# Routed sweep of an expert layer: the down weights are split inside the expert's own piece, between its up blocks

## Chip, cores and metric

One core of one Trainium2 chip. The metric is the device time of one execution of the whole kernel in microseconds; the times shown are the median of several executions, and the profile is of one execution more.

## What is computed

The reference normalises `x` (8 x 1024 tokens of 512 channels), runs a gated linear recurrence over it, and multiplies it by the SiLU of a mixture of 32 experts. What matters here is the routed part of that mixture:

```python
topk_ids = jnp.argmax(logits, axis=-1)             # one expert for each token
order = jnp.argsort(topk_ids)
sorted_x = (x * sigmoid(topk_val))[order]
g = ragged_dot(sorted_x, routed_gate_w, tokens_per_expert)   # 512 -> 1024
u = ragged_dot(sorted_x, routed_up_w, tokens_per_expert)     # 512 -> 1024
d = ragged_dot(silu(g) * u, routed_down_w, tokens_per_expert)  # 1024 -> 512
```

All values are float32. The kernel gets its precision by writing every operand as a rounded part `hi` plus a remainder `lo` and summing three products: hi x hi, hi x lo and lo x hi.

## The kernel before

The kernel has three sweeps, one after the other: the shared part of the mixture, the recurrence, and `routed_sweep`, which the change touches. The routed sweep fills the last third of the time, from about 2615 us of the profiled execution.

**Pieces.** The routed sweep walks over pieces. A piece is up to 384 tokens of one expert, as 8, 10 or 12 units of 32 tokens, so its matmuls have 256, 320 or 384 columns. An expert with more than 384 tokens has `full` whole pieces ahead of its last one; `full` is read from a table while the kernel runs, as are the number `p` of the first piece and the size `n` of the last. The last piece of an expert goes through `piece(p + full, e, n, split)`.

**What TensorE (PE) does in a piece.** There are eight blocks `b` of 128 hidden channels each. For each block it forms the gate product into `tG` (lines 87 to 89, 12 matmuls) and then the up product into `tU` (12 matmuls); each of the two has two banks, used in turn. Before the gate product of block b it waits for `sg_done`, that is for the SiLU of block b-2 on ScalarE (L1413), and before the up product for `h_done`, the product of block b-2 on VectorE (L1494). After block 6 it transposes the first 128 tokens of the piece that follows (`turn_x(p + 1, 0)`, L1558, into the one buffer `tX`). Then comes the down product (L1601), with two halves of the hidden channels: `down(0, 0)`, `turn_x(p + 1, 1)`, `down(0, 1)`, for a piece of more than 256 tokens `down(0, 2)`, then `turn_x(p + 1, 2)` or, where the next piece has only two groups of tokens, a bare wait in its place, and `down(1, g)` for all groups. Each `turn_x` waits until VectorE has emptied `tX` of the group before (`xlo`).

**What ScalarE (ACT) and VectorE (DVE) do in a piece.** For each block ACT computes `silu(b)` (L1413), DVE the product `h_mul(b)` (L1494), ACT the rounded copy `h_hi(b)` (L1422), DVE the remainder `h_lo(b)` (L1498). Both engines work strictly in the order in which the code lists the instructions. In block 7 the first transposed group is split too: ACT `x_hi` (L1401), DVE `x_lo` (L1469).

**The weights.** An expert's weights are six parts q of 1 MB each: q = 0 to 3 hold the gate and up columns of two blocks each, q = 4 (`D0`) and q = 5 (`D1`) the two halves of the down weights. A part is loaded by SyncE's queue (L1260, two transfers of 512 KB) into `raw[q % 3]`; ACT rounds it into `whi[q]` (`split_hi`, L1284), DVE takes the remainder into `wlo[q]` (`split_lo`, L1288). SyncE loads the parts in the order 0 to 5 and waits before each until the part three places earlier has been split, since that frees the raw buffer. `whi` and `wlo` have one buffer for each part.

**Where the splits stand.** Ahead of the sweep all six parts of expert 0 are split. In a piece of expert e (its last one) the parts of expert e+1 are split: q = 0 after block 2, q = 1 after block 4, on ACT q = 2 in block 6 and q = 3 after block 7, on DVE both after block 7; then `D0` after the x splits, and `D1` at the very end, after the output work of the piece (`gated`, L1452 on ACT; `total` and `result`, L1508, L1512 and L1515 on DVE). The next piece begins on ACT and DVE with register work: three table values (`order`, L1205) are read.

**The output** of a piece: DVE adds the shared part to `psY`, ACT takes the SiLU, DVE multiplies and adds, and GpSimd scatters the rows.

Of the kernel before, what the change touches and what calls it, by code (L numbers as in the profile page):

```python
# [1119 lines left out]
def routed_sweep(nc, z, x, rgw, ruw, rdw, xs_dram, ss_dram, tok_dram, orders, listed, ident, out):  # L1120
# [5 lines left out]
    KD, NI, D, E, T, NU = z.KD, z.NI, z.D, z.E, z.T, z.NU  # L1126
    GROUPS = PIECE // P
# [13 lines left out]
    with ExitStack() as ctx:  # L1141
# [84 lines left out]
            with eng.Else():  # L1226
                by_size(eng, n, body, sizes[:half])

        def experts(eng, piece):


            def expert(e, split):
                p = order(eng, FIRST_PIECE, e, 0, E + MOST)
                full = order(eng, FULL, e, 0, MOST)
                n = order(eng, LAST, e, LEAST, MOST_UNITS)
                with eng.If(full > 0):
                    with eng.Fori(0, MOST) as i:
                        with eng.If(full > i):
                            piece(p + i, e, MOST_UNITS, False)
                piece(p + full, e, n, split)  # L1240

            with eng.Fori(0, E - 1) as e:
                expert(e, True)
            expert(E - 1, False)

        def part(q, e):

# [34 lines left out]
        def split_hi(act, q, e):  # L1282
            act.wait_ge(raw_loaded[q], (e + 1) * 32)
            act.activation(whi[q][:], raw[q % RING][:], ACT.Copy).then_inc(whi_done[q], 1)  # L1284

        def split_lo(dve, q, e):
            dve.wait_ge(whi_done[q], e + 1)
            dve.tensor_tensor(wlo[q][:], raw[q % RING][:], whi[q][:], ALU.subtract).then_inc(wlo_done[q], 1)  # L1288
# [106 lines left out]
        @block.scalar  # L1395
        def _(act):
            act.sem_inc(sg_done, 2)

            def x_hi(p, g):
                act.wait_ge(turned_x, p * GROUPS + g + 1)  # L1400
                act.activation(xT[:, 0, :, turned(g)], psX[:], ACT.Copy).then_inc(xhi, 1)  # L1401

            split_hi(act, 0, 0)
            for g in range(GROUPS):
                x_hi(0, g)
            for q in range(1, PARTS):
                split_hi(act, q, 0)

            def piece(p, e, n, split):
                def silu(b):  # L1410
                    act.wait_ge(g_mm, p * NI + b + 1)
                    act.wait_ge(h_done, p * NI + b + 1)
                    act.activation(sg[b % 2][:], psG[b % 2][:, 0:PIECE], ACT.Silu).then_inc(sg_done, 1)  # L1413

                def h_hi(b):
                    act.wait_ge(h_done, p * NI + b + 3)
                    if b < KH:
                        act.wait_ge(d0_mm, p * 2 + 2)
                    else:
                        for g in range(GROUPS):  # L1420
                            act.wait_ge(y_mm[g], p + 1)
                    act.activation(hT[:, 0, b], h[b % 2][:], ACT.Copy).then_inc(hhi, 1)  # L1422

                def hi(q):
                    if split:
                        if q < D0:
                            act.wait_ge(u_mm, p * NI + 2 * q + 2)
                        elif q == D0:
                            act.wait_ge(d0_mm, p * 2 + 4)
                        else:  # L1430
                            for g in range(GROUPS):
                                act.wait_ge(y_mm[g], p + 2)
                        split_hi(act, q, e + 1)

                for b in range(NI):
                    silu(b)
                    if b == NI - 2:
                        hi(2)
                    if b == NI - 1:
                        act.wait_ge(u_mm, p * NI + NI)  # L1440
                        x_hi(p + 1, 0)
                    h_hi(b)
                    if b == 2 or b == 4:
                        hi(b // 2 - 1)
                hi(NQ - 1)
                for g in range(1, GROUPS):
                    x_hi(p + 1, g)
                hi(D0)

                def gated(g):  # L1450
                    act.wait_ge(z_done[g], p + 2)
                    act.activation(yo[g][:], yo[g][:], ACT.Silu).then_inc(zs_done[g], 1)  # L1452

                gated(0)
                gated(1)
                third(act, n, lambda: gated(2), lambda: act.sem_inc(zs_done[2], 1))
                hi(D1)

            experts(act, piece)

        @block.vector
        def _(dve):
            dve.sem_inc(h_done, 2)
            for g in range(GROUPS):
                dve.sem_inc(z_done[g], 1)

            def x_lo(p, g):
                dve.wait_ge(xhi, p * GROUPS + g + 1)
                dve.tensor_tensor(xT[:, 1, :, turned(g)], psX[:], xT[:, 0, :, turned(g)], ALU.subtract).then_inc(xlo, 1)  # L1469

            by_step = [t[:, 0:NU].rearrange("p (s n) -> p n s", n=STEP) for t in (scatter_at, gather_at)]
            numbers = psY[0][:, 0:NU].rearrange("p (n s) -> p n s", n=STEP)
            for bank in psG + psU:
                dve.memset(bank[:], 0.0).then_inc(cleared, 1)
            dve.wait_ge(returned, 16 * STEP)
            dve.tensor_copy(back, back_i).then_inc(back_done, 1)
            dve.wait_ge(turned_table, 1)
            dve.tensor_copy(by_step[0], numbers).then_inc(table, 1)
            dve.tensor_scalar(clipped, psY[0][:, 0:NU], float(T - 1), None, ALU.min).then_inc(table, 1)
            dve.memset(gather_at[:, NU:NU + 16], 0)  # L1480
            dve.memset(scatter_at[:, NU:NU + 16], T).then_inc(table, 1)
            dve.wait_ge(table, 3)
            dve.tensor_copy(by_step[1], clipped.rearrange("p (n s) -> p n s", n=STEP)).then_inc(table, 1)
            split_lo(dve, 0, 0)
            for g in range(GROUPS):
                x_lo(0, g)
            for q in range(1, PARTS):
                split_lo(dve, q, 0)

            def piece(p, e, n, split):  # L1490
                def h_mul(b):
                    dve.wait_ge(sg_done, p * NI + b + 3)
                    dve.wait_ge(u_mm, p * NI + b + 1)
                    dve.tensor_tensor(h[b % 2][:], sg[b % 2][:], psU[b % 2][:, 0:PIECE], ALU.mult).then_inc(h_done, 1)  # L1494

                def h_lo(b):
                    dve.wait_ge(hhi, p * NI + b + 1)
                    dve.tensor_tensor(hT[:, 1, b], h[b % 2][:], hT[:, 0, b], ALU.subtract).then_inc(hlo, 1)  # L1498

                def lo(q):  # L1500
                    if split:
                        split_lo(dve, q, e + 1)

                def total(g):
                    dve.wait_ge(y_mm[g], p + 2)
                    dve.wait_ge(ss_loaded[g], (p + 1) * 16)
                    dve.wait_ge(yo_free, p + 1)
                    dve.tensor_tensor(yo[g][:], psY[g][:], ss[g][:, 0:D], ALU.add).then_inc(z_done[g], 1)  # L1508

                def result(g):  # L1510
                    dve.wait_ge(zs_done[g], p + 1)
                    dve.tensor_tensor(yo[g][:], yo[g][:], ss[g][:, D:2 * D], ALU.mult).then_inc(zm_done[g], 1)  # L1512
                    dve.wait_ge(zm_done[g], p + 1)
                    dve.wait_ge(xr_loaded[g], (p + 1) * 16)
                    dve.tensor_tensor(yo[g][:], yo[g][:], xr[g][:], ALU.add).then_inc(yo_done[g], 1)  # L1515

                for b in range(NI):
                    h_mul(b)
                    if b == NI - 1:
                        x_lo(p + 1, 0)  # L1520
                    h_lo(b)
                    if b == 2 or b == 4:
                        lo(b // 2 - 1)
                lo(2)
                x_lo(p + 1, 1)
                lo(NQ - 1)
                x_lo(p + 1, 2)
                lo(D0)

                def absent():  # L1530
                    dve.sem_inc(z_done[2], 1)
                    dve.sem_inc(zm_done[2], 1)
                    dve.sem_inc(yo_done[2], 1)

                def last():
                    total(2)
                    result(2)

                total(0)
                total(1)  # L1540
                result(0)
                result(1)
                third(dve, n, last, absent)
                lo(D1)

            experts(dve, piece)

        @block.tensor
        def _(pe):
# [127 lines left out]
```

## Time and profile before

| | |
|---|---|
| median of 3 executions | 4001.32 us (3999.62 to 4002.64) |
| the profiled execution, own time | 3997.86 us |
| its span, first to last instruction | 3996.2 us |
| PE busy | 3867.3 us, 97% |
| DVE busy | 2083.3 us, 52% |
| ACT busy | 2018.7 us, 51% |
| mean granted TensorE clock | 0.988 |

The span leaves out what lies before the first and after the last instruction, 1.7 us here. Busy time of PE is the union of its matmuls, whose ends are modelled. A row of the timeline gives start, duration, engine, line, operation, the tile written and the tiles read, and in square brackets how long the engine had been idle before it and what ended that.

### The profile page before, as it was taken

The page shows a single profiled execution, that of the slowest core. Times are in us where ns is not written, and L with a number is a line of the kernel's source. Part 1 is how long each engine was busy: PE and PEld are TensorE (multiplying, and loading weights), DVE is VectorE, ACT ScalarE, POOL GpSimd, SP SyncE. Part 2 cuts the span into 40 slices and gives each one's busy share as a digit, 9 for nine tenths or more (in the row PEclk, how much of TensorE's full clock was granted, in tenths as well). Part 3 has the DMA queues.
Part 4 walks back from the last instruction along what each step waited for, and adds up shares of the span by engine and source line. Part 5 has one row for each costly group of instructions (what it writes and reads, how often), then busy time and mean ns, then how long its engine had stood idle before and what let it go on. Part 6 is the DMA issues. An engine that isn't in the chain of part 4 may idle for free. (4 is left out here: it accounts for less than half of the span.)

```text
span 3996.2 us, 57408 instructions
## 1 busy us (share of the span) xinstructions
PE 3867.3 (97%) x19586; PEld 3290.6 (82%) x19587; DVE 2083.3 (52%) x3048; ACT 2018.7 (51%) x2696; POOL 790.7 (20%) x840
## 2 busy tenths in 40 slices
PE   7999999999989999999999999959999999999998
PEld 5888888888867788888888888858999999998997
DVE  5232322323246655555555555556667767677674
ACT  3222222222227666676666666645455556555553
POOL 2011010111103200000000000024333434343433
PEclk9999999999989999999999999979999999999999
DMA  4212121121122000000010000066676767777673
GB/s 157 76 74 84 59 88 63 79 79 73 64 62 66 32 32 32 31 31 31 32 63 31 31 31 31 10 211 223 215 246 229 262 219 257 239 263 250 219 264 125
DMA packets 271955, 466.38 MB, mean 117 GB/s; under 512 B 23306, under 2 KB 171403, under 8 KB 268052
## 3 DMA queue, kind: packets, MB, share of 16 engines
q1 hardware_dynamic: 234276, 346.48, 25.3%
q0 software_dynamic: 37616, 119.08, 8.6%
q8 instruction: 37, 0.61, 0.1%
q14 instruction: 26, 0.21, 0.0%
HBM read 364.73 MB, written 102.99 MB: 117 GB/s over the span
## 5 line engine op out<-in xcount | busy, mean ns | idle before, releaser
L87 PE MATMUL gate<-xT,w_hi 128*128 128x512 f32 x1536 | 600.6, 391 | 1.9 <-DVE b2all L990 1.9
L88 PE MATMUL gate<-xT,w_hi 128*128 128x512 f32 x1536 | 600.5, 391 | 0.0
L89 PE MATMUL gate<-xT,w_lo 128*128 128x512 f32 x1536 | 598.9, 390 | 0.0
L1288 DVE TENSOR_TENSOR wlo<-raw,whi 128x2048 fp32r<-128x2048 f32 x192 | 439.6, 2289 | 127.8 <-ACT whi L1284 127.7
L529 DVE TENSOR_TENSOR h_act<-h_act,psU 128x512 f32<-128x512 f32 x128 | 88.0, 687 | 683.9 <-PE psU L89 683.8
L1601 PE MATMUL tY<-whi,thT 128*128 128x512 f32 x1264 | 410.7, 395 | 2.6 <-issue 2.4
L1284 ACT ACTIVATE whi<-raw 128x2048 fp32r<-128x2048 f32 x192 | 365.4, 1903 | 46.0 <-DMA raw<-in_L_ffn_routed_up_w 26.1
L87 PEld LDWEIGHTS gate<-xT,w_hi 128*128 128x128 f32 x1536 | 288.7, 188 | 67.1 <-DVE b2all L990 3.5
L89 PEld LDWEIGHTS gate<-xT,w_lo 128*128 128x128 f32 x1536 | 288.9, 188 | 62.1
L88 PEld LDWEIGHTS gate<-xT,w_hi 128*128 128x128 f32 x1536 | 288.7, 188 | 60.5
L87 PE MATMUL tG<-txT,whi 128*128 128x256 f32 (+2 forms) x1024 | 309.2, 302 | 25.6 <-ACT tsg L1413 12.8
L1034 DVE SCALAR_TENSOR_TENSOR log_f<-gate,b1s,log_f 128x512 f32<-128x512 f32 x128 | 96.1, 751 | 407.3 <-ACT log_f L931 407.3
L87 PE MATMUL tU<-txT,whi 128*128 128x256 f32 (+2 forms) x1024 | 305.7, 299 | 2.5 <-DVE th L1494 2.5
L89 PE MATMUL tG<-txT,wlo 128*128 128x256 f32 (+2 forms) x1024 | 304.9, 298 | 0.0
L88 PE MATMUL tG<-txT,whi 128*128 128x256 f32 (+2 forms) x1024 | 304.8, 298 | 0.0
L88 PE MATMUL tU<-txT,whi 128*128 128x256 f32 (+2 forms) x1024 | 304.7, 298 | 0.0
L89 PE MATMUL tU<-txT,wlo 128*128 128x256 f32 (+2 forms) x1024 | 304.6, 298 | 0.0
L1422 ACT ACTIVATE thT<-th 128x384 fp32r<-128x384 f32 x256 | 134.0, 523 | 302.8 <-DVE th L1494 302.8
L884 POOL COPY state<-hs 128x1 f32<-128x1 f32 x128 | 23.7, 185 | 1320.8 <-DVE hs L965 1320.8
L1601 PEld LDWEIGHTS tY<-whi,thT 128*128 128x128 f32 x1264 | 237.4, 188 | 54.3 <-issue 6.5
L431 ACT ACTIVATE h_act<-psG 128x512 f32<-128x512 f32 x128 | 76.5, 598 | 347.2 <-PE psG L89 345.4
L1601 PE MATMUL tY<-wlo,thT 128*128 128x512 f32 x632 | 246.4, 390 | 0.0
(210 smaller groups left out, 8913.4 us busy)
## 6 DMA issues: line engine op xcount, KB each, us to landing
raw<-in_L_ffn_routed_gate_w SPq DMA_DIRECT2D x128, 512.0 KB, 3.7
raw<-in_L_ffn_routed_up_w SPq DMA_DIRECT2D x128, 512.0 KB, 4.7
raw<-in_L_ffn_routed_down_w SPq DMA_DIRECT2D x128, 512.0 KB, 4.7
xT_dram<-xT SPq DMA_DIRECT2D x16, 2048.0 KB, 6.3
xT<-xT_dram SPq DMA_DIRECT2D x14, 2048.0 KB, 8.1
x_in<-in_L_attn_x SPq DMA_DIRECT2D x16, 1024.0 KB, 5.4
xs_dram<-x_in SPq DMA_DIRECT2D x16, 1024.0 KB
ss_dram<-y_sb SPq DMA_DIRECT2D x64, 256.0 KB, 2.1
```

Source lines behind the costliest of these rows:

```text
L87: pe.matmul(out, w[0], x[0], start=start, stop=False)
L88: pe.matmul(out, w[0], x[1], start=False, stop=False)
L89: return pe.matmul(out, w[1], x[0], start=False, stop=stop)
L431: act.activation(h[:, b % 2], psG[b % 2][:], ACT.Silu).then_inc(sg_done, 1)
L529: dve.tensor_tensor(h[:, b % 2], h[:, b % 2], psU[b % 2][:], ALU.mult).then_inc(h_done, 1)
L884: pool.tensor_copy(state[:, kb:kb + 1], hs[:, CHUNK - 1:CHUNK]).then_inc(state_done, 1)
L1034: dve.scalar_tensor_tensor(lf[:], bank(n, 0)[:], bias(GF, kb), lf[:], ALU.add, ALU.min)\
L1284: act.activation(whi[q][:], raw[q % RING][:], ACT.Copy).then_inc(whi_done[q], 1)
L1288: dve.tensor_tensor(wlo[q][:], raw[q % RING][:], whi[q][:], ALU.subtract).then_inc(wlo_done[q], 1)
L1422: act.activation(hT[:, 0, b], h[b % 2][:], ACT.Copy).then_inc(hhi, 1)
L1601: mm = pe.matmul(psY[g][:], hT[:, a, b, g * P:(g + 1) * P], w[q][:, kb, :], start=b == 0 and a == 0 and w is whi, stop=b == NI - 1 and a == 1)
```

## The change

On ACT and DVE the splits of the down parts D0 and D1 leave the end of the piece of the expert ahead. They are done in the expert's own first piece, D0 after block 0 and D1 after block 2 (`own_half`, under a branch on `full < 1`; where the expert has full pieces, they are done in front of these instead). The gate and up parts of the next expert move too: q = 0 from after block 2 to after block 3, q = 1 from after block 4 to after block 5, q = 2 on ACT from block 6 to after block 7; and the x splits of groups 1 and 2 stand now between q = 2 and q = 3 (ACT) or around q = 2 (DVE). Ahead of the sweep only q = 0 to 3 of expert 0 are split. The code of TensorE, SyncE and GpSimd is unchanged.

```diff
-        def experts(eng, piece):
+        def experts(eng, piece, own):
...
                 with eng.If(full > 0):
+                    for q in (D0, D1):
+                        own(p, e, q)
                     with eng.Fori(0, MOST) as i:
                         with eng.If(full > i):
-                            piece(p + i, e, MOST_UNITS, False)
-                piece(p + full, e, n, split)
+                            piece(p + i, e, MOST_UNITS, False, None)
+                piece(p + full, e, n, split, full)
...
+        def own_half(eng, own, p, e, q, full):
+            if full is not None:
+                with eng.If(full < 1):
+                    own(p, e, q)
...
@@ scalar
-            for q in range(1, PARTS):
+            for q in range(1, NQ):
                 split_hi(act, q, 0)
+            def own(p, e, q):
+                if q == D0:
+                    act.wait_ge(d0_mm, p * 2 + 2)
+                else:
+                    for g in range(GROUPS):
+                        act.wait_ge(y_mm[g], p + 1)
+                split_hi(act, q, e)
...
                 def hi(q):
                     if split:
-                        if q < D0:
-                            act.wait_ge(u_mm, p * NI + 2 * q + 2)
-                        elif q == D0:
-                            act.wait_ge(d0_mm, p * 2 + 4)
-                        else:
-                            for g in range(GROUPS):
-                                act.wait_ge(y_mm[g], p + 2)
+                        act.wait_ge(u_mm, p * NI + 2 * q + 2)
                         split_hi(act, q, e + 1)
                 for b in range(NI):
                     silu(b)
-                    if b == NI - 2:
-                        hi(2)
                     if b == NI - 1:
                         act.wait_ge(u_mm, p * NI + NI)
                         x_hi(p + 1, 0)
                     h_hi(b)
-                    if b == 2 or b == 4:
+                    if b == 0 or b == 2:
+                        own_half(act, own, p, e, D0 + b // 2, full)
+                    if b == 3 or b == 5:
                         hi(b // 2 - 1)
+                hi(2)
+                x_hi(p + 1, 1)
                 hi(NQ - 1)
-                for g in range(1, GROUPS):
-                    x_hi(p + 1, g)
-                hi(D0)
+                x_hi(p + 1, 2)
...
                 third(act, n, lambda: gated(2), lambda: act.sem_inc(zs_done[2], 1))
-                hi(D1)
@@ vector
-            for q in range(1, PARTS):
+            for q in range(1, NQ):
                 split_lo(dve, q, 0)
+            def own(p, e, q):
+                split_lo(dve, q, e)
...
                     h_lo(b)
-                    if b == 2 or b == 4:
+                    if b == 0 or b == 2:
+                        own_half(dve, own, p, e, D0 + b // 2, full)
+                    if b == 3 or b == 5:
                         lo(b // 2 - 1)
+                x_lo(p + 1, 1)
                 lo(2)
-                x_lo(p + 1, 1)
+                x_lo(p + 1, 2)
                 lo(NQ - 1)
-                x_lo(p + 1, 2)
-                lo(D0)
...
                 third(dve, n, last, absent)
-                lo(D1)
```

## Rows read from the trace of the kernel before

**Rows 1.** The page: span, and each engine's busy time, share, instructions.

```profile
span 3996.2 us, 57408 instructions
...
PE 3867.3 (97%) x19586; PEld 3290.6 (82%) x19587; DVE 2083.3 (52%) x3048; ACT 2018.7 (51%) x2696; POOL 790.7 (20%) x840
```

**Rows 2.** PE's waits from 2500 us on: total us, times, longest us.

```profile
PE tG L87 <- ACT tsg L1413: 12.8, 8, 7.5
...
PE tX L1558 <- DVE txT L1469: 8.7, 18, 1.5
...
PE tU L87 <- DVE th L1494: 2.5, 9, 0.3
```

**Rows 3.** Groups of PE by shape, from 2620 us on: first gate matmuls.

```profile
L87 PE MATMUL tG<-txT,whi 128*128 128x256 f32 x544 | 157.9, 290 | 22.1 <-ACT tsg L1413 12.8 <-issue 9.3
...
L87 PE MATMUL tG<-txT,whi 128*128 128x320 f32 x416 | 129.7, 312 | 3.5 <-issue 3.5
```

**Rows 4.** ACT's timeline in a piece of 256 columns, from its blocks.

```profile
3130.23 0.53 ACT L1422 ACTIVATE thT<-th 128x384 fp32r<-128x384 f32 x1 [1.55 <-DVE th L1494]
...
3133.47 0.52 ACT L1422 ACTIVATE thT<-th 128x384 fp32r<-128x384 f32 x1 [0.71 <-DVE th L1494]
3133.90 1.90 ACT L1284 ACTIVATE whi<-raw 128x2048 fp32r<-128x2048 f32 x1
3135.70 0.47 ACT L1413 ACTIVATE tsg<-tG 128x384 f32<-128x384 f32 x1
3138.62 0.52 ACT L1422 ACTIVATE thT<-th 128x384 fp32r<-128x384 f32 x1 [2.45 <-DVE th L1494]
...
3148.14 0.51 ACT L1422 ACTIVATE thT<-th 128x384 fp32r<-128x384 f32 x1
```

**Rows 5.** DVE's timeline, the same piece: its start, the first split.

```profile
3125.91 0.69 DVE L1515 TENSOR_TENSOR yo<-yo,xr 128x512 f32<-128x512 f32 x1
3126.51 2.29 DVE L1288 TENSOR_TENSOR wlo<-raw,whi 128x2048 fp32r<-128x2048 f32 x1
3129.56 0.55 DVE L1494 TENSOR_TENSOR th<-tsg,tU 128x384 f32<-128x384 f32 x1 [0.76 <-PE tU L89]
...
3135.82 2.29 DVE L1288 TENSOR_TENSOR wlo<-raw,whi 128x2048 fp32r<-128x2048 f32 x1 [1.25 <-ACT whi L1284]
```

**Rows 6.** PE's timeline: blocks 0 and 1 of that piece, its second transpose.

```profile
3123.05 0.28 PE L87 MATMUL tG<-txT,whi 128*128 128x256 f32 x1
...
3125.93 0.28 PE L87 MATMUL tG<-txT,whi 128*128 128x256 f32 x1
...
3150.36 0.66 PE L1558 MATMUL tX<-ident,xg 128*128 128x128 f32 x4 [0.36 <-DVE txT L1469]
```

**Rows 7.** PE's and ACT's timelines, the piece of 320 columns at 3205 us.

```profile
3205.57 0.30 PE L87 MATMUL tG<-txT,whi 128*128 128x320 f32 x1
...
3236.92 0.60 PE L1558 MATMUL tX<-ident,xg 128*128 128x128 f32 x4
...
3213.17 0.52 ACT L1422 ACTIVATE thT<-th 128x384 fp32r<-128x384 f32 x1 [0.97 <-DVE th L1494]
```

**Rows 8.** Timelines at the first piece: PE, then DVE.

```profile
2682.35 0.60 PE L1558 MATMUL tX<-ident,xg 128*128 128x128 f32 x4
...
2648.46 2.29 DVE L1288 TENSOR_TENSOR wlo<-raw,whi 128x2048 fp32r<-128x2048 f32 x1 [0.57 <-ACT whi L1284]
...
2656.49 2.29 DVE L1288 TENSOR_TENSOR wlo<-raw,whi 128x2048 fp32r<-128x2048 f32 x1 [2.62 <-ACT whi L1284]
2659.87 0.56 DVE L1494 TENSOR_TENSOR th<-tsg,tU 128x384 f32<-128x384 f32 x1 [1.08 <-ACT tsg L1413]
```

**Rows 9.** A stretch: us, busy time of each engine, PE clock, DMA share, GB/s.

```profile
2660.00:2670.00 10.00, 10.00 (x66) 10.00 (x66) 5.40 (x8) 4.51 (x7) 3.69 (x4) 0.74 0.95 345
```

**Rows 10.** ACT's table loads at L1413: duration min/median/max, first and last start.

```profile
L1413 ACT ACT_TABLE_LOAD  x31: 1283/1283/1283, 2657.3 to 3901.5; - x31
```

**Rows 11.** SyncE's queue, its waits from 2500 us on.

```profile
SPq L1260 <- DVE wlo L1288: 1076.5, 188, 12.9
```

More of the change, by code:

```diff
@@ L1405, in _, with piece @@
                 x_hi(0, g)
-            for q in range(1, PARTS):
+            for q in range(1, NQ):
                 split_hi(act, q, 0)
-            def piece(p, e, n, split):
+            def own(p, e, q):
[5 more added lines that the diff above has]
+                split_hi(act, q, e)
+            def piece(p, e, n, split, full):
                 def silu(b):
@@ L1456, in piece @@
                 third(act, n, lambda: gated(2), lambda: act.sem_inc(zs_done[2], 1))
-                hi(D1)
-            experts(act, piece)
+            experts(act, piece, own)
         @block.vector
@@ L1486, in _, with piece @@
                 x_lo(0, g)
-            for q in range(1, PARTS):
+            for q in range(1, NQ):
                 split_lo(dve, q, 0)
-            def piece(p, e, n, split):
+            def own(p, e, q):
+                split_lo(dve, q, e)
+            def piece(p, e, n, split, full):
                 def h_mul(b):
@@ L1543, in piece @@
                 third(dve, n, last, absent)
-                lo(D1)
-            experts(dve, piece)
+            experts(dve, piece, own)
         @block.tensor
```

## The prediction

> **What bounds the kernel now.** I read the page first: PE is busy for 97% of the span, ACT and DVE for about half of it [rows 1]. The kernel is bound by matmuls, and a change to ACT's and DVE's order can do two things only: take away waits of PE, or make new ones. So the next view is the list of what PE waits for from the last part of the recurrence on [rows 2]. The three waits that the change can reach are those for the SiLU (12.8 us, of which 7.5 are one wait in the first piece), for the emptied `tX` (8.7 us) and for `h_mul` (2.5 us): 24 us in all, and that is the ceiling of any gain, save for a clock effect below. Then I look at how large the pieces are. A piece has 8 x 4 = 32 gate matmuls of line 87, so the groups by shape give 544/32 = 17 pieces of 256 columns and 416/32 = 13 of 320 [rows 3]; with 32 experts and no expert in two pieces, the other 2 have 384. So `full` is 0 for all experts, and each piece will split its own down parts in its blocks 0 and 2. Last comes the timeline of one 256-column piece, where the answer lies [rows 4 to 6]. All times in it are counted from its first gate matmul at 3123.05.
>
> **The change, part by part.** The number of splits stays: 192 on each engine, none longer or shorter. The output work, the matmuls and the bytes loaded are the same. What changes is how many splits stand between the blocks.
>
> *A block with a split behind it.* ACT and DVE form one chain there: `h_hi(2)` starts at 3133.47, ACT's split at 3133.90 (1.90 us), DVE's at 3135.82 (2.29 us), only then can DVE do `h_mul(3)`, and `h_hi(3)` starts at 3138.62. From `h_hi` to `h_hi` that is 5.15 us [rows 4, 5]. Without a split it is 1.62: `h_hi(0)` at 3130.23, `h_hi(2)` at 3133.47, 3.24 for two [rows 4]. PE needs 2.88 us for a block of 256 columns (3123.05 to 3125.93 [rows 6]) and may be two blocks ahead of the chain, no more, since `tG` and `tU` have two banks.
>
> *Before*, the chain has two splits up to block 6. `h_hi(0)` starts at 7.18, `h_hi(6)` at 25.09 [rows 4], and `turn_x(p+1, 1)`, which needs the `x_lo` of block 7, at 27.31 after a wait of 0.36 [rows 6], 2.22 behind `h_hi(6)`. So in these pieces chain and PE are nearly level already.
>
> *After*, there are four: behind blocks 0 (D0), 2 (D1), 3 and 5. The chain is then 4 x 5.15 + 2 x 1.62 = 23.84 from `h_hi(0)` to `h_hi(6)`, and 26.06 with the 2.22 to `turn_x`. With `h_hi(0)` at 7.18 as before, `turn_x` starts at 33.24 and not at 27.31. That is 5.93 us late, and what PE does behind it (the rest of the down product) is its own work and comes later by as much. I count the piece by this one point because the waits inside it are all included: walking PE along the chain I get waits of about 1.2 us at the gate product of block 3 (it needs `silu(1)`, which stands behind the D0 split: 7.18 + 0.43 + 1.80 + 0.47 = 9.9, against 8.7), 1.0 at the up product of block 3 (`h_mul(1)` ends at 12.3), 0.9 at the up product of block 5, 1.3 and 1.0 at the two of block 6, and 1.4 at `turn_x`: 6.8, less the 0.65 or so of before, is the same again within 0.3. Of 17 such pieces 16 pay this (the first is worked out below): 16 x 5.93 = 94.9 us.
>
> *Pieces of 320 columns.* `turn_x` starts at 3236.92 - 3205.57 = 31.35, with no wait, and `h_hi(0)` at 7.60 [rows 7]. After: 7.60 + 26.06 = 33.66, 2.31 late. Where the piece ahead has only two groups of tokens, `h_hi(0)` can start as early as 7.18, which makes it 1.89. I take 2.1. The last piece splits only D0 and D1 and keeps its slack, so 12 pieces pay: 25.2 us. A piece of 384 columns needs about 384/320 of the block time, some 5.6 us more up to `turn_x`, and its chain is no longer: nothing.
>
> *The first piece.* Before, `silu(0)` and `h_mul(0)` stand behind the splits of D0 and D1: `h_mul(0)` starts at 2659.87, 3.38 after the last split's start at 2656.49. After, the last split ahead is that of q = 3, at 2648.46, so `h_mul(0)` can start at 2651.84, `h_hi(0)` at 2652.42, and with the chain of four splits `turn_x` at 2678.48. Before it started at 2682.35 [rows 8]. The 7.5 us wait goes, the splits between the blocks take half of it back: -3.9 us.
>
> *The start of the other pieces.* One split (D1) no longer stands between the output work and `silu(0)`, and D0 is gone from the down phase. I count this at nothing, since another thing covers it: the read of three table values, which goes on while that split runs. The split starts at 3126.51, 0.60 after the last output instruction's start, and `h_mul(0)` only at 3129.56, 0.76 after DVE is free again [rows 5]. Without the split these reads begin at most 0.6 sooner: bound -0.6 x 28 = -17 us. Against it stands the new branch, twice a piece on each engine, whose cost no row shows by itself. On DVE it lies in the 1.9 us in which DVE waits for `whi`; on ACT beside the 0.43 us of `h_hi`. From below it costs nothing; from above I set for both branches of a piece together the 0.76 that DVE loses at a piece's start, where it reads three table values and takes several branches [rows 5]: 28 x 0.76 = +21 us. Nearest is the place itself, under the 0.43 and the 1.9 us of cover, so I take zero for both.
>
> *Loads.* SyncE's code is the same, its waits move with the splits. They come late now by the dozen (1076.5 us in 188 waits [rows 11]), so the queue is idle for most of a piece. The shortest path after the change is q = 3: its raw buffer comes free in block 3 and it is needed after block 7, over 15 us for 1 MB; D1's comes free in the down phase and is needed after block 2. Nothing.
>
> **Sum.** 94.9 + 25.2 - 3.9 = 116.2 us. The profiled execution took 3997.9 us (span 3996.2), so 4114 for one like it; the median of the runs shown is 3.5 us longer: 4117 us.
>
> **A rule on the clock.** After the one wait of 7.5 us the granted clock was 0.74 in the stretch that followed [rows 9], a mixture of the two levels, 1.2 and 2.4 GHz; the other seven waits for the SiLU are (12.8 - 7.5) / 7 = 0.8 us each [rows 2], and the mean over the whole execution is 0.988, so they cannot each have cost such a stretch. The new waits are at most 1.4 us long but come six to a piece. The Trainium skill, "TensorE: Matmul & The Clock Gate", section "A second HAM failure mode: psum-queue depth-cycling", says that an engine that idles shortly and often between groups of matmuls can swing between both levels. No stretch here shows that; if it held, it is the second rival below.
>
> **The rivals.**
> - *The lead of PE swallows the splits* (faster). Place: between `h_hi(0)` and `turn_x` of each piece. It decides if the two more splits cost that chain nothing: 27.31 - 7.18 = 20.13 us are there, and 17.91 + 2.22 = 20.13 are used, with a wait of 0.36 already. Then PE would lose its waits for SiLU, `tX` and `h_mul`, up to 24 us less the first wait's share, and about 2.5 us more for the slow clock behind the first wait: 3981 at best. Against it: 5.15 between `h_hi` and `h_hi` with a split is the sum of its parts, 0.43 + 1.92 + 2.2 + 0.6, and it is made of instructions that wait for each other. 0.05.
> - *The clock swings* in the 256-column pieces: 0.74 over 10 us is 2.6 us lost; 16 x 2.6 = 42 on top: 4159. 0.04.
> - *Half is hidden*: were the 320-column pieces to pay nothing, and the 256-column ones half, because the chain catches up in blocks 6 and 7 more than it does in [rows 4], the sum is 47 - 4 = 43: 4045. For it speaks only that the chain was never seen with more than two splits; against it the same as above. 0.06.
> - *Nothing measurable*, the loss of the pieces being as small as the gain of the first: 4001. 0.02.
> - *A table load at each branch.* ACT loads its table once a piece (31 times 1283 ns [rows 10]). If the new branches made it load again before `silu(1)` and `silu(3)`, that SiLU would end 3.6 us after the split's start, and DVE is free of its own split only after 4.1: mostly hidden, within the range.
>
> **How the numbers follow.** The forecast has 0.83. Its own bounds are the -17 and +21 of the start and the branches, and 2.1 for 320 columns between 1.9 and 2.3 (12 x 0.2 = 2.4 either way): 4117 - 19 = 4098 to 4117 + 23 = 4140. Of the other cases those below lie far off; to leave out no more than 2 in 10 I go a little beyond these bounds, from 4085 to 4143. Faster and slower mean by more than 0.2% (8 us), about what a measurement of this kernel can tell from no change: faster 0.05, within 0.02, slower 0.93.
>
> **What would show it.** In the changed kernel's profile a 256-column piece should last 5.9 us longer than before, with `h_hi(0)` to `h_hi(1)` at 5.15, and `turn_x` at 33 behind the piece's first matmul; a 320-column piece some 2 us longer, a 384-column piece as long as before. PE's wait for `h_mul` should grow from 2.5 us to some 55, that for the SiLU to some 45, that for `tX` to some 30. The wait of 7.5 in the first piece should be gone. I am wrong if a piece starts much sooner than now (then the register work was no cover), if ACT and DVE step faster than 5.15 with a split, or if a wait for `whi` or for a raw buffer turns up.

## The result and the profile after

The changed kernel takes 4104.72 us (4102.65 to 4105.91, 4 runs) where the kernel before takes 4000.47 (3998.09 to 4002.64) in runs beside it. The ratio is 1.0263, with a 95% interval of 1.025 to 1.0276: 104 us slower. The forecast was 4117, 12 us too high. The profiled execution took 4105.19 us.

The page of the changed kernel:

```profile
span 4103.5 us, 57600 instructions
...
PE 3893.3 (95%) x19584; PEld 3294.7 (80%) x19587; DVE 2082.9 (51%) x3048; ACT 2013.3 (49%) x2696; POOL 800.9 (20%) x840
```

Beside [rows 1] the span is 107.3 us longer, and the counts and busy times of DVE and ACT are as they were, within 6 us. So none of their work became longer. PE waits more. Its waits from 2500 us on, in total, with their number and the longest:

```profile
PE tU L87 <- DVE th L1508: 41.1, 62, 0.7
PE tG L87 <- ACT tsg L1431: 37.9, 52, 1.1
PE tX L1572 <- DVE txT L1480: 29.6, 29, 1.5
```

These three were 2.5, 12.8 and 8.7 us [rows 2]; 24.0 have become 108.6, which is 85 of the 107 us. The other part stands in PE's busy time, 26 us longer with the same matmuls: busy time is counted to the modelled ends, and a wait begins there only. Where the waits come from is seen in one piece, the same one as in [rows 4 to 6]; its first gate product is now at 3149.36. ACT's timeline, `h_hi` (L1440) and the table load ahead of the first SiLU:

```profile
3153.06 1.28 ACT L1431 ACT_TABLE_LOAD   x1 [2.15 <-issue]
...
3156.54 0.53 ACT L1440 ACTIVATE thT<-th 128x384 fp32r<-128x384 f32 x1 [1.70 <-DVE th L1508]
3156.97 1.90 ACT L1294 ACTIVATE whi<-raw 128x2048 fp32r<-128x2048 f32 x1
...
3161.70 0.52 ACT L1440 ACTIVATE thT<-th 128x384 fp32r<-128x384 f32 x1 [2.45 <-DVE th L1508]
...
3163.31 0.52 ACT L1440 ACTIVATE thT<-th 128x384 fp32r<-128x384 f32 x1 [0.71 <-DVE th L1508]
...
3168.46 0.53 ACT L1440 ACTIVATE thT<-th 128x384 fp32r<-128x384 f32 x1 [2.45 <-DVE th L1508]
...
3173.76 0.52 ACT L1440 ACTIVATE thT<-th 128x384 fp32r<-128x384 f32 x1 [2.60 <-DVE th L1508]
3175.38 0.52 ACT L1440 ACTIVATE thT<-th 128x384 fp32r<-128x384 f32 x1 [0.71 <-DVE th L1508]
3180.53 0.53 ACT L1440 ACTIVATE thT<-th 128x384 fp32r<-128x384 f32 x1 [2.45 <-DVE th L1508]
```

From `h_hi(0)` to `h_hi(6)` the steps are 5.16, 1.61, 5.15, 5.30, 1.62 and 5.15: 23.99 us, where 17.91 were spent before [rows 4]. Each 5 us step has one split in it. PE's timeline of the piece:

```profile
3149.36 0.28 PE L87 MATMUL tG<-txT,whi 128*128 128x256 f32 x1
...
3161.72 0.38 PE L87 MATMUL tU<-txT,whi 128*128 128x256 f32 x1 [0.72 <-DVE th L1508]
...
3182.76 0.66 PE L1572 MATMUL tX<-ident,xg 128*128 128x128 f32 x4 [1.39 <-DVE txT L1480]
```

The up product of block 3 starts at 12.36 behind the first row, 0.02 after `h_hi(1)`: it waited for `h_mul(1)`. The second transpose starts at 33.40 where it was 27.31 [rows 6]. DVE's timeline, the start of the piece and `h_mul(4)`:

```profile
3152.21 0.69 DVE L1529 TENSOR_TENSOR yo<-yo,xr 128x512 f32<-128x512 f32 x1
3155.87 0.55 DVE L1508 TENSOR_TENSOR th<-tsg,tU 128x384 f32<-128x384 f32 x1 [2.97 <-PE tU L89]
...
3173.03 0.55 DVE L1508 TENSOR_TENSOR th<-tsg,tU 128x384 f32<-128x384 f32 x1
```

From the last output instruction to `h_mul(0)` it is 3.66 us; with the D1 split between them it was 3129.56 - 3125.91 = 3.65 [rows 5]. The split left and the time stayed: DVE is now idle for 2.97 of it. The one step that is 0.15 longer, behind block 3, is late at `h_hi(4)`: `h_mul(4)` ends at 3173.58 and `h_hi(4)` starts 0.18 behind that end.

I took the length of each piece from PE's timeline, from its first gate product to the next piece's, in both profiled executions. The differences make up the span's:

| what | pieces | us longer |
|---|---|---|
| 256 columns, behind a piece with two groups of tokens | 9 | 52.1 |
| 256 columns, behind a piece with three groups | 7 | 36.0 |
| 320 columns, without the last piece | 12 | 24.8 |
| 384 columns | 2 | 0.0 |
| the first piece | 1 | -3.1 |
| the last piece | 1 | 0.0 |
| what lies ahead of the first gate product (2643.77 to 2641.24) | | -2.5 |
| sum | | 107.3 |

The first piece, on PE's timeline of the changed kernel:

```profile
2641.24 0.57 PE L87 MATMUL tG<-txT,whi 128*128 128x256 f32 x1 [9.18 <-issue]
...
2653.49 0.39 PE L87 MATMUL tG<-txT,whi 128*128 128x256 f32 x1 [0.86 <-ACT tsg L1431]
...
2676.95 0.66 PE L1572 MATMUL tX<-ident,xg 128*128 128x128 f32 x4 [1.38 <-DVE txT L1480]
```

The wait of 7.5 us for the first SiLU has shrunk to 0.86, and `turn_x` starts at 2676.95 instead of 2682.35 [rows 8].

### The profile page after: what moved, and what is told of

It is laid out like the page before. It is cut to its first block and busy times, and to the rows that moved or that the text cites. A ratio compares the mean times of both kernels' runs of the same rounds, so it can differ in the third digit from the quotient of the medians.

```text
span 4103.5 us, 57600 instructions
## 1 busy us (share of the span) xinstructions
PE 3893.3 (95%) x19584; PEld 3294.7 (80%) x19587; DVE 2082.9 (51%) x3048; ACT 2013.3 (49%) x2696; POOL 800.9 (20%) x840
## 5 line engine op out<-in xcount | busy, mean ns | idle before, releaser
L1294 ACT ACTIVATE whi<-raw 128x2048 fp32r<-128x2048 f32 x192 | 364.7, 1900 | 25.6 <-DMA raw<-in_L_ffn_routed_up_w 25.6
L1440 ACT ACTIVATE thT<-th 128x384 fp32r<-128x384 f32 x256 | 134.3, 525 | 414.0 <-DVE th L1508 414.0
```

## The experiments

Each was timed beside the kernel before. The first four kernels were timed beside runs of it with a median of 3996.8 us, the other four beside 3996.2, so the ratios compare better than the times. Losses and gains by pieces come from the profiled executions, measured as in the table above.

### The same splits in pairs

```diff
-                    if b == 0 or b == 2:
-                        own_half(act, own, p, e, D0 + b // 2, full)
-                    if b == 3 or b == 5:
-                        hi(b // 2 - 1)
+                    if b == 2:
+                        own_half(act, own, p, e, D0, full)
+                        own_half(act, own, p, e, D1, full)
+                    if b == 5:
+                        hi(0)
+                        hi(1)
```

DVE likewise.

> The changed kernel with the same four splits between the blocks, but D0 and D1 both behind block 2 and q = 0 and 1 both behind block 5. Theory (the chain h_hi to h_hi sets the piece): with two splits in a row ACT's second runs beside DVE's first, so such a step takes 5.15 + 2.20 = 7.35 us and not 5.15 + 5.15 - 1.62 = 8.68 for the two; from h_hi(0) to h_hi(6) 2 x 7.35 + 4 x 1.62 = 21.2 instead of 23.84, and PE, two blocks ahead, loses some 2.7 us less in a 256-column piece (about 3 us over the kernel before) and all of the 2 us in a 320-column piece: 4105 - 16 x 2.7 - 12 x 1.9 = 4039. Rival (every split between the blocks costs PE the same, wherever it stands): 4105. Rival (the loss comes from D0 and D1 no longer being covered by the down phase, not from the chain between the blocks): 4105.

Measured: 4062.35 us (4056.36 to 4064.45), ratio 1.0165 (1.0148 to 1.0182). By the ratios (1.0263 to 1.0165) that is 39 us less than the changed kernel, where both rivals expected nothing and the theory 66. ACT's timeline of the same piece:

```profile
3138.47 0.52 ACT L1440 ACTIVATE thT<-th 128x384 fp32r<-128x384 f32 x1 [0.71 <-DVE th L1510]
3138.90 3.70 ACT L1294 ACTIVATE whi<-raw 128x2048 fp32r<-128x2048 f32 x2
...
3145.82 0.52 ACT L1440 ACTIVATE thT<-th 128x384 fp32r<-128x384 f32 x1 [2.85 <-DVE th L1510]
```

The step with two splits is 7.35 us, to the hundredth what was worked out, and the 320-column pieces lose only 6.2 us together. So the number of splits alone does not set the loss, and neither does the mere absence of D0 and D1 from the down phase. The rest of the missing gain is a thing that the theory left out. PE's timeline of that piece at `turn_x`:

```profile
3158.79 1.11 PE L1576 MATMUL tX<-ident,xg 128*128 128x128 f32 x4 [2.32 <-DVE txT L1482]
3159.56 0.78 PE L1619 MATMUL tY<-whi,thT 128*128 128x512 f32 x1
3160.13 0.63 PE L1619 MATMUL tY<-wlo,thT 128*128 128x512 f32 x1
```

and two stretches, of this kernel behind that wait of 2.32 us and behind the same wait in the piece at 3047.78:

```profile
3158.00:3163.00 5.00, 4.21 (x14) 3.56 (x15) 3.27 (x5) 3.95 (x4) 0.00 (x0) 0.66 1.06 369
...
3077.50:3082.50 5.00, 4.18 (x20) 3.43 (x21) 3.27 (x5) 4.81 (x5) 0.00 (x0) 1.00 0.88 310
```

In the first the granted clock is 0.66, part of it at the lower of the two levels (1.2 of 2.4 GHz), and the down product runs at 0.63 us for a matmul, not 0.39. In the second, behind a wait just as long, it stays at 1.00. The slow stretch is there in 11 of the 17 pieces of 256 columns. It costs some 1.5 us: pieces behind a three-group piece take 39.3 to 39.7 us without it and 40.8 to 40.9 with it, and those behind a two-group piece, nearly all with it, 41.0 to 41.5. By pieces, the 256-column pieces behind the first are 25.6 us shorter than in the changed kernel where 43 were expected, and eleven times 1.5, some 16 us, is nearly the whole of that miss. The 320-column pieces are 18.6 us shorter where 23 were expected; the first piece and what lies ahead of it are 4.5 shorter, which was not expected. So the profiled execution is 49 us faster than the changed kernel's. It was the fastest of four; the others took 5 to 8 us longer, and no trace shows why. ACT's waits for `raw`, in 13 places more than in the changed kernel and 8 us together, may have a part in what is left.

The 256-column pieces of the changed kernel, the first left aside, have no such stretch; their waits end at 1.39:

```profile
3182.00:3187.00 5.00, 4.24 (x23) 3.61 (x24) 3.27 (x5) 4.86 (x5) 0.00 (x0) 1.00 0.51 176
```

The changed kernel has one slow stretch, though, at the start of its third piece, of 320 columns, where PE stood still for 2.80 us, and not for ACT or DVE:

```profile
2731.33 0.41 PE L87 MATMUL tG<-txT,whi 128*128 128x320 f32 x1 [2.80 <-issue]
...
2731.00:2736.00 5.00, 4.67 (x21) 4.68 (x22) 0.87 (x2) 1.77 (x2) 2.27 (x2) 0.66 0.44 159
```

The kernel before stood still for 3.49 us in that place and kept its clock at 1.00.

### DVE's part of the own splits cut short

```diff
+            dve.wait_ge(whi_done[0], 1)
+            for q in (D0, D1):
+                dve.tensor_tensor(wlo[q][:], whi[0][:], whi[0][:], ALU.subtract)
...
             def own(p, e, q):
-                split_lo(dve, q, e)
+                dve.wait_ge(whi_done[q], e + 1)
+                dve.tensor_tensor(wlo[q][:, :, 0:64], raw[q % RING][:, :, 0:64], whi[q][:, :, 0:64],
+                                  ALU.subtract).then_inc(wlo_done[q], 1)
```

The first three lines set both remainders to zero once, ahead of the sweep. The kernel leaves out seven eighths of each.

> The changed kernel, with DVE's subtraction for D0 and D1 cut to an eighth of its columns (the rest of those remainders is left at zero; ACT's part, the loads and all waits stay). Theory: behind a D split h_mul waits for ACT's 1.80 us and the SiLU only, so that step falls from 5.15 to 0.43 + 1.80 + 0.50 + 0.60 = 3.35 us; 1.8 us less for each of two steps, 3.6 in a 256-column piece, and a 320-column piece loses nothing any more: 4105 - 16 x 3.6 - 12 x 1.9 = 4024. Rival (the branches or ACT's split alone set the loss): 4105, at most a few us less.

Measured: 4019.36 us (4019.29 to 4020.57), ratio 1.0056 (1.004 to 1.0073), 83 us below the same kernel with the whole subtraction, which at its ratio of 1.0263 is 4102 beside 3996.8. ACT's timeline around the first own split:

```profile
3127.84 0.53 ACT L1440 ACTIVATE thT<-th 128x384 fp32r<-128x384 f32 x1 [1.69 <-DVE th L1513]
...
3131.26 0.53 ACT L1440 ACTIVATE thT<-th 128x384 fp32r<-128x384 f32 x1 [0.71 <-DVE th L1513]
```

The step is 3.42 us instead of 5.16. The 256-column pieces behind the first lose 31.1 us instead of 88.1, which is 3.56 less each where 3.6 was expected, and those of 320 columns 0.8 instead of 24.8. ACT's splits, the branches and the loads are all still there, so the part of the loss that is gone with it belongs to DVE's subtraction, which stands in front of `h_mul`.

### Without the branches

```diff
-                with eng.If(full < 1):
-                    own(p, e, q)
+                own(p, e, q)
```

> The changed kernel without the branches around the own D splits (right only where no expert has more than 384 tokens, as here). Theory: the branches lie under h_hi and under DVE's wait for whi, so 4105 within 2 us. Rival (the new branches are part of the loss): up to 0.38 us for each of 56 on a piece's path, 4084.

Measured: 4098.44 us (4097.2 to 4099.94), ratio 1.0253 (1.0236 to 1.027). The time alone does not tell it from the changed kernel, since the intervals overlap. The trace does. ACT's `h_hi(0)` and `h_hi(6)` in the same piece:

```profile
3153.53 0.53 ACT L1439 ACTIVATE thT<-th 128x384 fp32r<-128x384 f32 x1 [1.70 <-DVE th L1507]
...
3177.36 0.53 ACT L1439 ACTIVATE thT<-th 128x384 fp32r<-128x384 f32 x1 [2.45 <-DVE th L1507]
```

They are 23.83 us apart, against 23.99 with the branches and 23.84 in the forecast. The 0.15 is gone from the step behind block 3: `h_hi(4)` starts here 0.04 behind the end of `h_mul(4)`, not 0.18. By pieces the span is 101.5 us longer than before and not 107.3: 2.3 us less in the 256-column pieces, 2.3 in those of 320, 1.5 in the first. So in the 28 pieces behind the first that lose time the branches cost 4.6 us, about 0.16 a piece, and not up to 0.76.

### Both gate and up splits behind the blocks

```diff
-                    if b == 3 or b == 5:
-                        hi(b // 2 - 1)
-                hi(2)
+                hi(0)
                 x_hi(p + 1, 1)
-                hi(NQ - 1)
+                hi(1)
                 x_hi(p + 1, 2)
+                hi(2)
+                hi(NQ - 1)
```

DVE's part moves in the same way.

> The changed kernel with q = 0 and 1 taken out from between the blocks and put behind block 7, so only D0 and D1 stand between the blocks, as many as in the kernel before, and q = 0 to 3 all follow the blocks. Theory with the down phase counted: DVE has four splits (8.8 us) and two x remainders between the last h_lo and the output work, total(0) comes some 3 us later than in the kernel before, h_hi(0) of the next piece with it, near 10 us behind the piece's start and not 7.2; the 320-column pieces lose too: about 4105 to 4110. Rival (only the number of splits between the blocks counts): that of the kernel before, about 4000.

Measured: 4146.02 us (4144.81 to 4148.36), ratio 1.0374 (1.0357 to 1.0392). As many splits between the blocks as in the kernel before, and the slowest kernel of all: the rival falls, and the theory was too mild by some 40 us. One thing that it left out is on ACT's timeline, at the last of the four:

```profile
3159.39 1.91 ACT L1294 ACTIVATE whi<-raw 128x2048 fp32r<-128x2048 f32 x1 [4.18 <-DMA raw<-in_L_ffn_routed_up_w]
```

Part q = 3 is loaded into the raw buffer that q = 0 leaves. With q = 0 split only behind block 7, its load starts there too, and ACT waits 4.18 us for it. `h_hi(0)` of the next piece is at 12.79, not near 10. The output work stands behind it, then the next piece's first SiLU, and PE's waits are in the place that the delay of `h_hi(0)` reaches:

```profile
PE tG L87 <- ACT tsg L1431: 102.6, 33, 5.1
...
PE tX L1572 <- DVE txT L1480: 1.5, 1, 1.5
```

The 320-column pieces lose 51 us here, double what they do in the changed kernel. The clock has a share too: the mean granted clock of this execution is 0.976, where it is 0.989 in the changed kernel. Between the first and the last piece it was at its lower level in 24 stretches of 3.4 or 6.8 us, 116 us together, each beginning within or just behind an idle time of PE of 2.6 to 5.1 us. At half the clock that is a loss of at most 58 us. How much of the 40 is the load's and how much the clock's was not separated.

### Three splits between the blocks

As before, but `q = 0` stays behind block 3, and only `q = 1` moves behind block 7:

```diff
-                    if b == 3 or b == 5:
-                        hi(b // 2 - 1)
+                    if b == 3:
+                        hi(0)
+                hi(1)
+                x_hi(p + 1, 1)
                 hi(2)
-                x_hi(p + 1, 1)
```

> The changed kernel with q = 1 taken from behind block 5 to behind block 7; three splits stay between the blocks. Theory: the chain is one split shorter (3.5 us), but DVE's output work comes later by a split, so the next piece's h_hi(0) moves from 7.2 to about 8; a 256-column piece loses some 1 us less than in the changed kernel: 4105 - 19 = 4086. The kernel with all four behind block 7 had also a wait for the load of q = 3; here its buffer comes free in block 3, so none is expected. Rival (each split between the blocks costs 2.95 us of a 256-column piece, nothing else does): 4058.

Measured: 4081.73 us (4080.27 to 4083.69), ratio 1.0215 (1.0199 to 1.0231), which is 4087 beside a kernel before of 4000.5: the theory's 4086, not the rival's 4058. In the piece of [rows 4 to 6] `h_hi(0)` comes at 8.19 instead of 7.18, as expected, and `h_hi(6)` at 28.64 instead of 31.17, so the end of the chain is 2.5 us earlier. The second transpose is only 0.53 earlier, at 32.88. PE's last wait in the blocks ends 25.3 us into the piece, and what it has to do from there to the transpose takes 7.6 us by itself. So PE's waits for `tX` go nearly wholly (1.5 us are left, in one wait). Cutting the chain shorter than that gives nothing back.

### DVE's subtraction behind the next product

```diff
                 for b in range(NI):
                     h_mul(b)
+                    if b == 1 or b == 3:
+                        own_half(dve, own, p, e, D0 + b // 2, full)
+                    if b == 4 or b == 6:
+                        lo(b // 2 - 2)
...
                     h_lo(b)
-                    if b == 0 or b == 2:
-                        own_half(dve, own, p, e, D0 + b // 2, full)
-                    if b == 3 or b == 5:
-                        lo(b // 2 - 1)
```

> The changed kernel, the same four splits between the blocks, ACT's order untouched; on DVE each subtraction stands behind h_mul of the next block and not in front of it. Theory (the loss is h_mul, h_hi and x_lo queued behind DVE's 2.2 us): h_mul(b+1) then waits for ACT's split and the SiLU only, PE's waits for h_mul go, and only the chain over two blocks, about 6.45 us instead of 5.15 + 1.62 = 6.77, and the x remainder at the end stay late; by the rows' durations some 2.7 us less in each 256-column piece and all of it in the 320-column pieces: 4040. Rival (it is the number of splits or the busy time between the blocks that costs): 4105, as the same work stands between the same blocks.

Measured: 4034.96 us (4032.29 to 4036.47), ratio 1.0096 (1.0081 to 1.0112), or 4039 beside a kernel before of 4000.5, where 4040 was expected. The work between the blocks is the same to the instruction; one change of order on one engine took 64% of the loss away. PE's waits:

```profile
PE tX L1572 <- DVE txT L1480: 30.9, 19, 2.4
PE tG L87 <- ACT tsg L1431: 27.9, 58, 1.1
```

Those for `h_mul` are gone, and the 320-column pieces lose 2.3 us in all, the whole of it in one piece, the third.

### The same order in the kernel before

```diff
                 for b in range(NI):
                     h_mul(b)
+                    if b == 3 or b == 5:
+                        lo(b // 2 - 1)
...
-                    if b == 2 or b == 4:
-                        lo(b // 2 - 1)
```

> The kernel before, with DVE's subtractions for q = 0 and 1 behind h_mul of the next block and not in front of it; nothing else changed. Theory: PE's 0.3 us waits for h_mul and 0.36 us waits for the emptied tX in the 256-column pieces go, the wait for the SiLU behind three-group pieces stays: about 16 x 0.55 = 9 us less, 3992 where the kernel before has 4000.5. Rival (those waits are too short to matter, the time goes elsewhere): no change.

Measured: 3978.4 us (3977.07 to 3982.12), ratio 0.9957 (0.9944 to 0.9971), 18 us faster by the medians where 9 were expected, twice what the waits in the rows add up to. What the list of waits leaves out is seen on PE's timeline of the kernel before, at the up product of block 7 in the piece of [rows 6]:

```profile
3144.99 0.28 PE L89 MATMUL tG<-txT,wlo 128*128 128x256 f32 x1
3145.55 0.39 PE L87 MATMUL tU<-txT,whi 128*128 128x256 f32 x1 [0.29 <-DVE th L1494]
3145.78 0.28 PE L88 MATMUL tU<-txT,whi 128*128 128x256 f32 x1
```

Matmuls of this shape start every 0.12 us. Here one starts 0.56 behind its predecessor, and the one after it 0.23 behind it: 0.55 us are lost, where the row counts 0.29, since it counts from the modelled end of the matmul ahead. With the new order the stretch up to the down product is 23.50 us instead of 24.04 in that piece, and the down part 11.86 instead of 12.58.

### And the first piece as in the changed kernel

```diff
+            expert(0, True, True)
-            with eng.Fori(0, E - 1) as e:
+            with eng.Fori(1, E - 1) as e:
                 expert(e, True)
...
+                    if full is not None and b in (0, 2):
+                        with act.If(full < 1):
+                            own(D0 + b // 2)
+                    if b in ((2, 4) if full is None else (3, 5)):
                         hi(b // 2 - 1)
```

DVE's part is changed in the same way, one `h_mul` later. Here `full` is handed to the first expert's piece alone, and only q = 0 to 3 are split ahead of the sweep.

> The same as the run before it, and in the first piece alone the splits as in the changed kernel (D0 behind block 0, D1 behind block 2, q = 0 and 1 behind blocks 3 and 5, DVE's part one h_mul later), with a piece of code of its own for expert 0; all other pieces as in the kernel before. Theory: the wait of 7.5 us in the first piece and the slow clock behind it go, some 5 us more than the run before it: 3986. Rival (what the first piece gains is lost in code of its own or in its four splits): as the run before it.

Measured: 3968.97 us (3962.15 to 3972.25), ratio 0.9927 (0.9914 to 0.9941), 27 us faster than the kernel before in the same batch, where the changed kernel's ratio is 1.0263. The first piece takes 41.58 us, 47.21 in the run before it: the expected 5 us. Another 4 us come from a thing that was not meant. Two groups of ACT's instructions, first of the run before it, then of this one:

```profile
L1413 ACT ACT_TABLE_LOAD x31 | 39.8, 1283 | 22.1 <-issue 22.1
```

```profile
L1420 ACT ACT_TABLE_LOAD x1 | 1.3, 1283 | 0.5 <-issue 0.5
```

With a first piece of its own ahead of the loop, only one of the 31 table loads is left. The 256-column pieces behind a three-group piece, which had waited 0.77 us for the first SiLU, are 0.5 us shorter. The profiled execution, 3972.25 us, is the slowest of the five: one of its 256-column pieces is 2.6 us longer than in the kernel of the run before, behind a wait of ACT of 3.04 us for the load of D0.

## Why the prediction was right, step by step

**The chain.** Shown. The steps of 5.15 and 1.62 came back as 5.15 to 5.30 and 1.61 to 1.62, the sum as 23.99 (23.83 without the branches) where 23.84 was worked out, and `turn_x` at 33.40, not 33.24. That it is this chain and not the count of splits is shown from three sides: the pairs (7.35), the short subtraction (3.42) and the changed order.

**The 256-column pieces.** The term was 94.9 us, measured 88.1: the mechanism was right, the size 7 too high. Nine pieces behind a two-group piece lost 5.8 each, near the forecast 5.93. The seven behind a three-group piece lost 5.14. I had worked out one piece of the first kind and taken it for all; the second kind began later before, and starts sooner now. ACT's timeline at the piece whose first gate product is at 3065.25:

```profile
3069.49 1.28 ACT L1431 ACT_TABLE_LOAD   x1 [2.14 <-issue]
...
3072.24 0.53 ACT L1440 ACTIVATE thT<-th 128x384 fp32r<-128x384 f32 x1 [0.97 <-DVE th L1508]
```

`h_hi(0)` is at 6.99, and the same piece of the kernel before had it at 7.60 (3057.34, behind a first gate product at 3049.74), after a table load at 4.83 where it is now 4.24. So the bound of -0.6 us for the absent D1 split was met where the piece ahead has three groups, and nothing was won where it has two (3.65 and 3.66 us). I had taken zero for both.

A second step was a little off, at both ends. The transpose is 6.1 us later in the piece of [rows 4 to 6], 0.15 more than forecast. But behind it not all came later by as much: the part behind the transpose is 9.30 us before and 9.16 after there, and in the pieces followed by one with two groups 9.15 and 8.75.

**The 320-column pieces**: 25.2 worked out, 24.8 measured, and in part that is luck. Behind a three-group piece 2.31 was worked out for each and 1.9 came, since the chain starts sooner there; behind a two-group piece 1.89 was worked out and 2.1 came, since the chain is 0.15 longer; and the third piece of the sweep lost 2.6, with the slow stretch of above in it. **384 columns and the last piece**: nothing, as said. **The first piece**: -3.9 worked out, -3.1 measured. **Ahead of it**: the first gate product is 2.5 us earlier, which the sum didn't have. It is there already at the last matmul of the recurrence, at 2618.35 us instead of 2621.42, for the same code of the sweeps ahead, so no wait of the routed sweep makes it. In the profiled executions of the seven kernels with the changed pieces the first gate product lies between 2638.6 and 2641.5, in those of the three others between 2642.7 and 2643.8. Whether this is scatter or comes with the changed code stays open.

**The 12 us.** Of what the forecast was too high, 7 us are the 256-column pieces, 2.5 what lies ahead, and some 3 the profiled executions: they are 107.3 us apart, the medians 104.

**The branches**: zero taken, 0.16 us a piece measured, 4 to 5 of the 107 us. **The loads**: hidden, as said; no wait for `raw` in the pieces of the changed kernel. The kernel with all four splits behind the blocks shows how near that limit is.

**The waits of PE** were forecast as 55, 45 and 30 us and came as 41, 38 and 30. They are low for the reason shown above: the rows count from a modelled end. There are 108 waits more than before (143 for 35), and the 26 us by which PE's busy time grew make a quarter of a microsecond for each.

**The rivals.** The clock did not swing in the 256-column pieces of the changed kernel: its mean is 0.989, 0.988 before, and the one slow stretch behind the first piece is that of the third piece, behind 2.80 us. Whether such waits can do it was worth asking, though: the pairs show it with waits of 2.3 us, in most pieces but not in all. That much of the section "A second HAM failure mode: psum-queue depth-cycling" in the Trainium skill's "TensorE: Matmul & The Clock Gate" is seen here, but no waits of 1.4 us and below, however often, did it in the changed kernel. The table load at each branch did not come: there are as many ACT instructions as before, 2696. That half is hidden or nothing measurable is left is refuted by the 104 us. That PE's lead would swallow the splits is refuted in the pieces of 256 and 320 columns by every run; in those of 384 columns it did, as was worked out.

## What to carry to other kernels

Where one engine runs at most two blocks ahead of a chain over two others, measure the chain from one of its instructions to the same one of the next block, with and without the extra work, and multiply; the share of busy time (here 52%) says nothing on it. Work that must go between the blocks goes behind the instruction that the bound engine waits for, not in front of it. And work that hides under something else, as one split did here under the reading of registers, gives nothing back when it is moved away.

## What the runs showed of the hardware

A wait of 2.3 us of PE was followed by a stretch at a lower clock in 11 of 17 pieces and not in the other six, in one execution and with the same instructions around it. The waits of up to 1.4 us in the changed kernel never were. At the start of the third piece 2.80 us of idle time were, in the changed kernel, and 3.49 us were not, in the kernel before. A wait in the list costs PE more than its row: 0.55 us for one of 0.29. Of the 31 table loads of 1.28 us in the sweep, in the kernel before and in the changed one, 30 were followed by the SiLU after 0.01 us; the Trainium skill, "ScalarE: Activation LUTs", section "What ACT_TABLE_LOAD costs", has 1283 ns for the load, as here, and a drain of about 1380 ns besides, which no row here shows: the shortest idle time ahead of a load was 0.48 us.
